# Attention steps of two head pairs in place of one: P V of both pairs in one PSUM bank, one raw copy for both, and the output projection spread over two iterations

## What is computed

```python
h = rms_norm(x, norm_weight)            # x: layer-normed input
q, k, v = split(h @ w_qkv.T)            # 16 heads of 64
q, k = apply_rope(q), apply_rope(k)     # t * cos + rotate_half(t) * sin
k, v = concat([pm, k]), concat([pm, v]) # 4 persistent keys and values
attn = softmax(where(causal, q @ k.T * scale, lowest))
out = (attn @ v) @ w_out.T
# second block, over the 32 batches x_t:
ft = sigmoid(xt @ wf.T + c @ uf.T + bf); it = sigmoid(xt @ wi.T + c @ ui.T + bi)
gt = tanh(xt @ wc.T + c @ uc.T + bc);    c = ft * c + it * gt
h = tanh(einsum('tbi,oi->tbo', x, wo) + c_final @ uo.T + bo)
```

## Time and profile before

| | |
|---|---|
| median of 3 runs | 1204.35 us (1203.41 to 1206.22) |
| the profiled execution, its own time | 1204.28 us |
| its span, first to last instruction | 1202.5 us |
| PE busy | 1136.8 us, 95% of the span |
| DVE / ACT / POOL busy | 942.5 / 684.7 / 655.0 us |
| granted TensorE clock, mean | 0.977 |

### The profile page before, as it was taken

One profiled execution on the slowest core, in us unless ns is written; L12 is line 12 of the kernel. 1 busy time (PEld: TensorE's weight loads), 2 busy tenths in 40 slices (PEclk: granted clock), 3 DMA queues, 4 the chain that ended last, 5 costly groups with the idle time before them and its releaser, 6 DMA issues.

```text
span 1202.5 us, 36709 instructions
## 1 busy us (share of the span) xinstructions
PE 1136.8 (95%) x13099; PEld 802.8 (67%) x13099; DVE 942.5 (78%) x3302; ACT 684.7 (57%) x1474; POOL 655.0 (54%) x1082
## 2 busy tenths in 40 slices
PE   3889999999999999999999999999999999999981
PEld 2556767667776766777677677767667777766661
DVE  5677888888877888787878878877788878788636
ACT  3555565656555566655656665565555565565533
POOL 3544555556555555655555556555556556555425
PEclk8899999999999999999999999999999999999995
DMA  5222333332233333233333323333332333333204
GB/s 200 86 83 79 108 104 112 107 108 83 84 104 98 116 106 109 70 96 106 99 115 109 107 73 92 105 108 108 104 97 78 98 108 95 112 103 97 65 10 140
DMA packets 77990, 119.80 MB, mean 100 GB/s; under 512 B 13041, under 2 KB 35954, under 8 KB 77682
## 3 DMA queue, kind: packets, MB, share of 16 engines
q1 hardware_dynamic: 68722, 111.18, 30.7%
q10 hardware_dynamic: 9088, 6.29, 1.8%
HBM read 41.53 MB, written 8.78 MB: 42 GB/s over the span
## 4 chain that ended last, share of the span: by engine, by line
PE 76%; DVE 6%; DMA 5%; ACT 4%; issue 4%; POOL 3%; SPq 2%; DVEq 0%; ACTq 0%; POOLq 0%
PE bank_pv L1044 13%; PE bank_st L1007 12%; PE bank L953 12%; PE bank_sum L1080 8%; PE bank L971 6%; PE bank_sum L1063 6%; PE bank_sm L985 5%; DMA rope_c<-rope_b 4%; PE bank_st L1010 3%; PE bank L1166 2%; PE bank L1168 2%; ACT xn L600 2%; PE bank_sm L993 2%; POOL qk L385 2%; PE bank L1095 1%
## 5 line engine op out<-in xcount | busy, mean ns | idle before, releaser
L385 POOL TENSOR_TENSOR qk<-rope_a,rope_c 128x512 f32<-128x512 f32 x256 | 336.0, 1312 | 269.7 <-DMA rope_c<-rope_b 264.5
L763 DVE CUSTOM_DVE_ANT_0 masked<-bank_sm,mask_q 128x132 bf16<-128x132 f32 (+1 forms) x1024 | 307.6, 356 | 43.5 <-PE bank_sm L985 42.9
L521 ACT ACTIVATE prob<-bank_st 128x776 f32<-128x776 f32 x256 | 208.5, 814 | 160.0 <-PE bank_st L1010 159.2
L752 DVE TENSOR_TENSOR rope_a<-bank,cos 128x512 f32<-128x512 f32 x256 | 174.1, 680 | 125.1 <-PE bank L953 116.2
L1007 PE MATMUL bank_st<-qk 64*128 64x256 f32 (+1 forms) x2048 | 239.4, 326 | 0.1
L376 POOL TENSOR_SCALAR_AFFINE_SELECT prob<-prob 128x256 f32<-128x256 f32 x256 | 113.9, 445 | 227.5 <-ACT prob L521 226.4
L1044 PE MATMUL bank_pv<-prob,v_sb 128*64 128x256 f32 (+1 forms) x2048 | 224.7, 340 | 2.2 <-POOL prob L378 1.8
L506 ACT ACTIVATE qk_h<-qk 128x512 f16<-128x512 f32 x256 | 160.1, 625 | 98.0 <-POOL qk L385 96.9
L1007 PEld LDWEIGHTS bank_st<-qk 64*128 64x128 f32 x2048 | 154.8, 188 | 31.7 <-issue 0.8
L753 DVE TENSOR_TENSOR rope_b<-bank,sin 128x512 f32<-128x512 f32 x256 | 173.7, 679 | 0.0
L1044 PEld LDWEIGHTS bank_pv<-prob,v_sb 128*64 128x64 f32 x2048 | 124.5, 136 | 72.7 <-issue 31.4
(11 more groups left out here) (190 smaller groups left out, 1712.5 us busy)
## 6 DMA issues: line engine op xcount, KB each, us to landing
rope_c<-rope_b SPq DMA_DIRECT2D x512, 128.0 KB, 2.1
rinv<-linv_scratch SPq DMA_DIRECT2D x124, 256.0 KB, 4.5
out<-x_sb SPq DMA_DIRECT2D x16, 256.0 KB, 2.5
linv_scratch<-linv SPq DMA_DIRECT2D x62, 64.0 KB, 2.0
x_sb<-x ACTq DMA_DIRECT2D x28, 128.0 KB, 4.8
pre<-w_qkv_t ACTq DMA_DIRECT2D x1, 1024.0 KB, 5.5
v_sb<-pm_v SPq DMA_DIRECT2D x64, 8.0 KB
v_end<-v_end_scratch SPq DMA_DIRECT2D x64, 8.0 KB
```

The costliest lines, as they stand in the source:

```text
L385: G.tensor_tensor(qk[:, s, :].rearrange("p (u n) -> p u n", u=2)[:, :, 0:NT], rope_a[:, s % 4, :].rearrange("p (u n) -> p u n", u=2), rope ...
L521: A.activation(prob[:, s % 4, :, :], ps_st[:, :, 0:SCOL], ACT.Exp).then_inc(S["exp_done"], 1)
L752: V.tensor_tensor(rope_a[:, s % 4, :], proj_bank(j, s)[:, :], cos[:, :], ALU.mult)
L763: ins = V.tensor_tensor_reduce(masked[:, e, c0:c0 + n], ps_sm[:, e, c0:c0 + n], mask_q[:, c0:c0 + n], 1.0, LOWEST, ALU.add, ALU.max, top[: ...
```

## The change

Line numbers of the changed kernel are those printed by the listing of its order; pieces keep their names.

- An iteration has 4 steps m of two pairs. On PE a step is: scores of one pair (`scores_for_max` of an odd pair, `scores_t(2m)`); then all that uses the full matrix (`values`, `project(2m)`, `project_out` or gates or transposes, `project(2m+1)`); then scores again (`scores_for_max` of an even pair, `scores_t(2m+1)`); then `attend` for both pairs of the step before, and `sums` of the same two pairs.
- `attend(bj, g)` writes two pairs side by side into `ps_pv`; one `raw_copy` of 512 columns takes both. The tail of P V (keys 256 to 259) goes to `ps_work` instead of `ps_pv`; ACT copies it to the new `tail_sb`, POOL adds it (`tail_add`) instead of DVE.
- `values` part 3 and the second part of the gates go through `ps_pv` instead of `ps_work`.
- `project_out` is split: parts 0 and 1 of batch j-2 in step 3 of iteration j, parts 2 and 3 in step 0 of iteration j+1, where `residual` and `rstd` now also stand. `second_norm` and `transpose_xn` move from the border of two iterations to step 1.
- Every engine's body is rewritten in steps m.

```diff
@@ POOL, ACT @@
+            def tail_add(cj):
+                pool.wait_ge(S["tail_read"], cj + 1)
+                pool.wait_ge(S["raw_done"], NDUO * cj + NDUO)
+                G.sem_inc(S["pool_tick"], 1)
+                o = raw[:, cj % 2, :, QE:NT]
+                G.tensor_tensor(o, tail_sb[:, :].rearrange("p (s n) -> p s n", s=NPAIR), o, ALU.add).then_inc(S["end_added"], 1)
...
-                A.activation(raw[:, par, s, :], ps_pv[:, 0:NT], ACT.Copy, scale=1.0 / RS).then_inc(S["raw_done"], 1)
+                A.activation(raw[:, bj % 2, 2 * g:2 * g + 2, :].rearrange("p s n -> p (s n)"), ps_pv[:, :], ACT.Copy,
+                             scale=1.0 / RS).then_inc(S["raw_done"], 1)
...
+            def tail_copy(bj):
+                act.wait_ge(S["tail_ready"], bj + 1)
+                wait(act, S["end_added"], bj)
+                A.activation(tail_sb[:, :], ps_work[:, 0:NPAIR * NEND], ACT.Copy, scale=1.0 / RS).then_inc(S["tail_read"], 1)
@@ ACT, body @@
+                for m in range(NDUO):
+                    if m < 2 and c:
+                        raw_copy(j - 2, m + 2)
+                    if m >= 2 and b:
+                        raw_copy(j - 1, m - 2)
+                    if m == 1 and c:
+                        tail_copy(j - 2)
+                    if b:
+                        exp(j - 1, 2 * m)
...
+                    if m == 1 and b:
+                        value_copy(j - 1, 2)
+                    if m == 1 and a:
+                        hi(j, 1)
+                    if m == 1 and d:
+                        second_norm(j - 3)
+                    if m == 1 and b:
+                        value_copy(j - 1, 3)
                         copy_top(j - 1, 1)
@@ DVE, body @@
+                for m in range(NDUO):
+                    if m < 2 and b:
+                        maxima(j - 1, 2 * m + 5)
+                    if m >= 2 and a:
+                        maxima(j, 2 * m - 3)
                     if a:
+                        rotate(j, 2 * m)
+                    if m == 0 and n:
                         first_stats(j + 1)
+                    if m == 0 and d:
+                        residual(j - 3)
+                    if m == 1 and c:
                         invert(j - 2)
+                    if m == 2 and c:
                         divide(j - 2, p, 0)
                         divide(j - 2, p, 1)
...
+                    if m == 0 and b:
+                        maxima(j - 1, 6)
+                    if m >= 1 and a:
+                        maxima(j, 2 * m - 2)
...
                     if a:
+                        rotate(j, 2 * m + 1)
@@ PE, attend and body @@
+            def attend(bj, g):
+                pe.wait_ge(S["causal_done"], NPAIR * bj + 2 * g + 2)
+                wait(pe, S["raw_done"], NDUO * bj + g)
...
+                for s in (2 * g, 2 * g + 1):
+                    o = s % 2 * NT
+                    for kc, q0, c0 in CHUNKS:
+                        for e in range(2):
+                            col = (2 * s + e) * DH
+                            last = T.matmul(ps_pv[OWN[e], o + q0:o + NT], v_sb[:, kc, col:col + DH],
+                                            prob[:, s % 4, e, c0:c0 + NT - q0], start=(kc == 0), stop=(kc == 1))
+                last.then_inc(S["pv_ready"], 1)
...
+                for m in range(NDUO):
+                    if m < 2 and b:
+                        scores_for_max(j - 1, 2 * m + 5)
+                    if m >= 2 and a:
+                        scores_for_max(j, 2 * m - 3)
                     if b:
+                        scores_t(j - 1, 2 * m)
...
                     if a:
+                        project(j, p, 2 * m)
+                    if m == 0 and d:
+                        project_out(j - 3, 1 - p, 2)
+                        project_out(j - 3, 1 - p, 3)
+                    if m == 1 and b:
+                        values(j - 1, 1 - p, 3)
                         transpose_top(j - 1, 1)
...
+                    elif m == 1 and d:
                         transpose_xn(j, j - 3)
...
                     if a:
+                        project(j, p, 2 * m + 1)
...
+                    if m >= 1 and b:
+                        attend(j - 1, m - 1)
+                        sums(j - 1, m - 1)
```

More of the change, by code:

```diff
@@ L294, in tail_values @@
             def tail_values(bj):
[L296 removed]
+                wait(sp, S["tail_ready"], bj)
                 sp.sem_inc(S["sp_tick"], 1)
@@ L653, in body @@
-                    if s == 7 and c:
-                        second_norm(j - 2)
-                    if j == 0 and s == 4:
+                    if j == 0 and m == 2:
                         mask_cast()
-                    if isinstance(j, int) and j == 1 and s == 4:
+                    if j == 1 and m == 2:
                         late_casts()
@@ new lines, in body @@
+                    if m >= 1 and a:
+                        maxima(j, 2 * m - 2)
+                    if j == 0 and m == 2:
+                        end_low()
+                    if a:
+                        rotate(j, 2 * m + 1)
+                    if m == 1 and d:
+                        xt_low(j - 3)
+                    if m == 2 and n:
+                        h_low(j + 1, 1 - p)
+                    if m == 2 and d:
+                        state(j - 3, 0)
+                    if m == 3 and b:
@@ L883, in body @@
                         end_sum(j - 1)
-                    if s == 6 and c:
-                        residual(j - 2)
-                    if s == 6 and d:
+                    if m == 3 and d:
                         state(j - 3, 2)
+                    if j == 1 and m == 3:
+                        scan_starts()
             iterations(nc.vector, body)
@@ L1029, in scores_t @@
                 last.then_inc(S["st_ready"], 1)
[L1031 to L1046 removed]
+            def attend(bj, g):
+                pe.wait_ge(S["causal_done"], NPAIR * bj + 2 * g + 2)
+                wait(pe, S["raw_done"], NDUO * bj + g)
+                if g == 0:
+                    pe.wait_ge(S["v_done"], 4 * bj + 4)
+                if g == 1:
+                    wait(pe, S["gate_read"], 2 * (bj - 2) + 2)
+                if g % 2 == 0:
+                    pe.wait_ge(v_pm[g // 2], 16 * (bj + 1))
+                for s in (2 * g, 2 * g + 1):
[6 more added lines that the diff above has]
+                last.then_inc(S["pv_ready"], 1)
+                if g == NDUO - 1:
@@ L1211, in body @@
-                    if s < 3 and b:
-                        scores_for_max(j - 1, s + 5)
-                    if s >= 3 and a:
-                        scores_for_max(j, s - 3)
-                    if b:
-                        scores_t(j - 1, s)
-                    if s == 0 and c:
-                        attend(j - 2, NPAIR - 1)
-                    if s >= 1 and b:
-                        attend(j - 1, s - 1)
-                    if s == 0 and c:
+                    if m == 1 and c and j - 2 == NB - 1:
+                        for i in range(4):
+                            spread_last(i)
@@ new lines, in body @@
+                    if j == 1 and m in (1, 2):
+                        end_values(m - 1)
+                    if m == 2 and d and j - 3 < NB - 1:
+                        gates(j, j - 3, 1)
+                    if m == 2 and n:
+                        transpose_x(j + 1)
+                    if m == 3 and a:
+                        transpose_top(j, 0)
+                    if m == 3 and c:
+                        project_out(j - 2, p, 0)
+                        project_out(j - 2, p, 1)
+                    if a:
+                        project(j, p, 2 * m + 1)
@@ L1222, in body @@
+                    if m == 0 and b:
+                        scores_for_max(j - 1, 6)
+                    if m >= 1 and a:
+                        scores_for_max(j, 2 * m - 2)
+                    if b:
+                        scores_t(j - 1, 2 * m + 1)
+                    if m == 0 and c:
+                        attend(j - 2, 3)
                         sums(j - 2, 3)
-                    if s in (2, 4, 7) and b:
-                        sums(j - 1, (2, 4, 7).index(s))
-                if isinstance(j, int) and j == 2:
+                    if m >= 1 and b:
+                        attend(j - 1, m - 1)
+                        sums(j - 1, m - 1)
```

278 lines of the change are left out of this document (116 added, 162 removed).

## The result

The changed kernel takes 1312.65 us (median of four runs, 1310.7 to 1316.95) against 1205.28 for the kernel before in the same job: a ratio of 1.0897 (95% interval 1.0865 to 1.0929). The direction was right and the size was not: 1259 was forecast, and the range ended at 1292. The profiled execution has a span of 1311.5 us against 1202.5.

What follows compares the result with a forecast made beforehand. The prediction took PE as the bound, busy 991 of 1000 us. Per iteration 33.5 + 2.3 + 0.9 = 36.7 us against 34.8, +1.9 over 29 iterations, gave +55 us: 1259 us, range 1217 to 1292.

Steps and rivals of the forecast that it cites:

- PE's floor: PE's work in an iteration without the new waits, 33.5 us after savings from 34.8.
- The wait at the transpose: In step 1, PE's `transpose_xn` waits for ACT behind the rope chain of pair 1: 2.3 us an iteration.
- (a): Step 2: PE's `project(j, 5)` waits for DVE's rotation of the single bank, 0.3 us.
- (b): Late `spread_linv` broadcast delays DVE's divide, so step 3's `transpose_top` waits 0.5 us.
- (c): `hi(j, 5)` and `copy_top` reach PE's scores about 0.1 us late.
- the smaller waits: Waits (a) to (c) behind the one at the transpose: together 0.9 us an iteration, nothing to 2 us possible.
- Rival 4: New waits lower PE's granted clock to a mean of 0.9: +3.7 us an iteration on the forecast, 1365 us; chance 0.05.
- Base and ends: Base of 34.8 us an iteration over 29 iterations; nothing taken for the kernel's start and end.
- Rival 1: Only the transpose wait remains, (a) to (c) vanish: +0.5 to +1.0 us an iteration, 1219 to 1233 us; chance 0.22.
- Rival 2: Waits chain more heavily, steps 2 and 3 lose 2 us and more: +3.0 an iteration, 1291 us; chance 0.13.
- Rival 3: Faster: 34.5 us an iteration or below, or 1166 us with the transpose fully hidden; chance 0.15.
- the seams: PE's tiling changes fall from 28 to 20 an iteration, saving 0.8 us; joined P V entries save 0.2.

Runs made afterwards that it cites:

- run 8: Changed kernel with `hi(j, 1)` moved behind `xt_high` on ACT and further reordering on ACT, PE and DVE: 1185.24 us, ratio 0.982 to the kernel before.
- run 1: Changed kernel with only `hi(j, 1)` moved on ACT, from ahead of `second_norm` to behind `xt_high`: 1250.62 us.
- run 9: Run 8 with `hi(j, 1)` put back ahead of `second_norm` on ACT: 1320.83 us.
- run 2: Changed kernel with eighteen unused matmuls on PE ahead of the transpose's wait for `xn`: 1306.2 us.
- run 11: Run 9 with `value_copy(j-1, 2)` ahead of `hi(j, 1)` on ACT again: 1283.24 us.
- runs 6 to 8: Run 1 with reordering added in turn on ACT, then PE and ACT, then DVE: 1244.7, 1225.82 and 1185.24 us.
- run 4: Changed kernel with `rotate(j, 1)` ahead of `maxima(j-1, 6)` on DVE: 1265.05 us.

## Why the prediction was right in direction and wrong in size

- **PE's floor, 33.5: right.** Adding each block's usual distance gives 33.6 in the changed kernel. P V of two pairs takes 1.46 with its change of tiling (1.36 with its tail behind it, 1.38 was taken), sums with their change 0.80. The unseen kinds, scores to full matrices and sums to scores, cost 0.09 to 0.10 like those of the earlier trace rows. Run 8 runs at 34.33 with these seams.
- **The wait at the transpose, 2.3: right.** 2.26 by the list of waits, 2.4 as distance; its chain is the one predicted, and moving its one instruction removes it (run 1) or brings it back (run 9).
- **(a), 0.3: right** (0.32). **(b) and (c), 0.6: too small.** (b) is 0.59 for 0.5, (c) 0.32 for 0.1, and about 0.3 of small waits were not listed. Together the smaller waits are 1.6 us for 0.9. The range's "nothing to 2 us" held them.
- **What PE loses beside that one wait: the step that failed.** The forecast took 0.9 for it: (a) to (c), and nothing for the clock. Measured are 2.6: 1.6 of smaller waits and 1.0 in blocks at half clock. Filling the idle time shows how much of this hangs on the clock: in run 2, with 0.1 us of half clock, 38.26 less the 33.6 and the 2.4 still leaves 2.3. So the clock was worth 0.3 us an iteration in this kernel; without it the smaller waits would have been more than twice the 0.9, and 1306.2 lies outside the range as well.
- **The clock, set to nothing.** Rival 4 priced a mean clock of 0.9 at 3.7 us and gave it 0.05, with the argument that PE "would still be busy for over 90% of an iteration and wait at most 2.3 us at a stretch". Busy share was indeed 91%, and the mean wait as long as that (single ones up to 3.1); the clock fell all the same, briefly, behind single waits. It was a term of the forecast's own case, 1.0 us an iteration in its blocks, and not a rival. The Trainium skill (TensorE: Matmul & The Clock Gate, Why this matters for your kernels) says that idle gaps between bursts can bring the low level. The trace agrees: half clock for 3.4 us after a gap of 2.98, and in 19 of the 28 iterations after gaps of 1.9 to 3.1.
- **Base and ends.** The sum compared 36.7 with 34.8, the mean of 30 intervals of which the last two are short; a full iteration before is 35.07. That made the forecast 0.27 an iteration too high. And "Start and end hold the same chains in the same order; I take nothing for them" missed 10.4 us. In run 8 too, where PE waits little, the first transpose comes at 122.0 instead of 110.5; what follows the 29th is 8.1 shorter than before there. That leaves 3.4 us for the moved work in the orders of run 8, and some 7 of the 10.4 for the waits in start and end.

The sum as it should have been: 33.6 + 2.4 + 1.0 + 1.6 = 38.6 us, less 35.07, times 28, is +99, and 10 in start and end.

These terms are not prices that can be taken off one by one. Removing the 2.4 and the 1.0 in the changed kernel brought 2.1 (run 1); putting `hi(j, 1)` into a kernel with hardly any other waits cost 4.6 (run 9), or 3.3 with the copy of v ahead of it as in the changed kernel (run 11 against run 8). Behind PE's wait DVE catches up, so that part of each later wait stands for the same lateness. Rival 1, that the 2.3 us would give DVE time and make (a) to (c) vanish, had this mechanism right, and its place wrong: the smaller waits shrank under the large one, but did not go. Rival 2, that steps 2 and 3 lose 2 us and more, did not come about: all the smaller waits together are 1.6. Rival 3's floor was there to be had as well: with the orders of ACT, PE and DVE fitted to the new steps, the kernel is 1.8% faster than before (run 8, 0.9799 to 0.984). The new orders were not tried on the kernel before, but they could give it little: PE was idle there for 9.1 us of 1000, 0.3 an iteration, and in run 8 for 15.9. PE's busy time in an iteration is 34.75 before (35.07 times 0.991) and 33.78 in run 8 (34.33 times 0.984), 1.0 less, as much as the prediction took for the seams. Of the 109 us, 62 go with the one f16 copy ahead of the second norm (run 1); what waited in its shadow went with the orders of runs 6 to 8.

## What to carry to other kernels

Where each engine's order is written by hand, follow for every moved instruction what stands directly ahead of it on its own engine and what that waits for. A busy share of 52% on ACT says nothing of a copy that waits 2.4 us for POOL, and through it for a DMA, at the head of the queue. When a wait of some two microseconds appears on PE, add a clock term to it (here 0.3 to 0.6 us an iteration, by how many other waits were ready to take it back), and test a suspect by moving that one instruction: then look for the waits that come out from behind it before believing any single price.

## What the hardware showed that was not expected

- Single idle stretches of PE of 1.9 to 3.1 us were followed by about 3.4 us at half clock in 19 of 28 iterations of the changed kernel; it was no matter of length alone, since after 1.87 us it fell and after 3.05 us it did not. In run 4, with waits of 0.9 to 1.5 us, it stayed at full, and fell once, after a wait of 1.95 us.
- With waits of the same length the falls come and go between executions of the same kernel: run 11 has 1.46 us at half clock an iteration in its profiled execution, which was also its fastest (1278.93). Its five executions follow the mean granted clock: 0.966, 0.963 and 0.961 took 1278.93, 1282.2 and 1283.24 us, 0.952 and 0.95 took 1295.33 and 1294.99. Run 8, which has no such waits, scatters by 2 us. A kernel with such waits measures less sharply.
- In run 9 the first matmul that is longer (0.42 us for 0.27) starts 0.36 us after PE resumes (524.53 after 524.17); in the changed kernel's window above it was at least 1.1 us.
